# Attention over edges in order of target: a group of 14 tiles as two halves of 64 rows

## The reference

```python
xp = (x @ lin_w).reshape(N, HEADS, HEAD_DIM)
a_i = jnp.einsum('nhc,hc->nh', xp, att_i)
a_j = jnp.einsum('nhc,hc->nh', xp, att_j)
alpha = a_i[dst] + a_j[src]
alpha = jnp.where(alpha >= 0, alpha, NEG_SLOPE * alpha)
amax = jax.ops.segment_max(alpha, dst, num_segments=N)
ex = jnp.exp(alpha - amax[dst])
denom = jax.ops.segment_sum(ex, dst, num_segments=N)
alpha = ex / (denom[dst] + SOFTMAX_EPS)
msg = xp[src] * alpha[:, :, None]
out = jax.ops.segment_sum(msg, dst, num_segments=N)
...
out = (out - mu) * jax.lax.rsqrt(var + LN_EPS) * ln_w + ln_b
out = jax.nn.elu(out)
return out + x
```

## Time and profile before

| what | us |
|---|---|
| median of 3 runs | 4499.56 |
| lowest, highest | 4498.87, 4500.8 |
| span of the profiled execution | 5824.1 |
| PE busy, in it | 4650.5 |
| DVE busy | 3605.8 |
| POOL busy | 3218.0 |
| ACT busy | 1536.9 |
| mean granted clock of TensorE | 0.863 |

### The profile page before, as it was taken

The page is one execution under the profiler, slowest core; times in us unless marked ns, Lnnn a source line. Parts: engine busy times, 40 slices in busy tenths (PEclk is TensorE's granted clock), DMA queues, the critical chain, the costliest instruction groups (busy, mean ns, idle before and its releaser), DMA issues. The chain is left out here.

```text
span 5824.1 us, 116189 instructions
## 1 busy us (share of the span) xinstructions
PE 4650.5 (80%) x33992; PEld 2943.9 (51%) x33992; DVE 3605.8 (62%) x10598; ACT 1536.9 (26%) x3203; POOL 3218.0 (55%) x3385
## 2 busy tenths in 40 slices
PE   6888888888888888888847777777777777777777
PEld 4444444444444444444435665555556555565555
DVE  3566666666666666666526666666666666666666
ACT  3121222212222222222213333333333333333333
POOL 3555555555555555555445555555555555555552
PEclk8999999999999999999967777777777777777777
DMA  6444444444444444444433333333333333333331
GB/s 228 126 127 122 132 125 127 129 123 135 122 130 127 125 132 122 130 126 124 135 94 95 90 93 94 93 92 91 94 92 91 94 93 93 93 92 94 95 92 52
DMA packets 410283, 649.87 MB, mean 112 GB/s; under 512 B 138008, under 2 KB 270442, under 8 KB 410204
## 3 DMA queue, kind: packets, MB, share of 16 engines
q0 software_dynamic: 161120, 444.76, 27.5%
q1 hardware_dynamic: 249084, 204.19, 11.6%
HBM read 546.95 MB, written 101.68 MB: 111 GB/s over the span
## 5 line engine op out<-in xcount | busy, mean ns | idle before, releaser
L977 POOL DMA_INDIRECT sub_xg<-y_rows,sub_meta x1668 | 1599.1, 959 | 1208.1 <-PE sub_a L1027 558.7
L2342 POOL DMA_INDIRECT ord_xg<-xpa_rows,ord_meta x1666 | 1597.6, 959 | 1201.8 <-PE ord_a L2410 548.0
L2410 PE MATMUL ord_a<-ord_xg,ord_sel 128*128 128x264 f32 x3332 | 1330.0, 542 | 91.5 <-DVE ord_xg L2773 66.5
L1027 PE MATMUL sub_a<-sub_mids,sub_sel 128*32 128x128 f32 (+1 forms) x13344 | 1119.7, 312 | 311.8 <-issue 215.3
L2410 PEld LDWEIGHTS ord_a<-ord_xg,ord_sel 128*128 128x128 f32 x3332 | 834.9, 275 | 255.8 <-DVE ord_xg L2773 76.1
L1347 DVE TENSOR_TENSOR sub_mids<-sub_w,sub_xg 128x256 f32<-128x256 f32 x834 | 351.1, 421 | 983.7 <-remote 790.2
L1027 PEld LDWEIGHTS sub_a<-sub_mids,sub_sel 128*32 128x32 f32 x13344 | 463.0, 110 | 810.8 <-issue 545.8
L1352 DVE TENSOR_TENSOR sub_mids<-sub_w,sub_xg 128x384 f32<-128x384 f32 x1668 | 844.4, 548 | 0.0
L2358 PE MATMUL ord_s<-ident,ord_sel 128*128 128x128 f32 x1666 | 348.2, 337 | 569.7 <-ACT ord_sel_t L2476 539.6
L1007 PE MATMUL sub_w<-sub_fc,sub_ht 64*128 64x256 f32 x3336 | 611.8, 438 | 11.0 <-issue 10.7
L2358 PEld LDWEIGHTS ord_s<-ident,ord_sel 128*128 128x128 f32 x1666 | 244.3, 172 | 709.5 <-issue 684.5
(11 more groups left out here) (206 smaller groups left out, 4433.2 us busy)
## 6 DMA issues: line engine op xcount, KB each, us to landing
sub_sum_rows<-sub_agg_s SPq DMA_DIRECT2D x556, 64.0 KB
sub_node_rows<-sub_sum_rows SPq DMA_DIRECT2D x49, 640.0 KB, 5.6
sub_xg<-y_rows,sub_meta POOLq DMA_INDIRECT x1668
ord_xg<-xpa_rows,ord_meta POOLq DMA_INDIRECT x1666
ord_x_rows<-x_rows SPq DMA_DIRECT2D x119, 128.0 KB
out_dram<-ord_res SPq DMA_DIRECT2D x119, 128.0 KB
xpa_rows<-sub_proj SPq DMA_DIRECT2D x49, 264.0 KB, 2.2
lin_xt<-in_x_t_dram SPq DMA_DIRECT2D x14, 896.0 KB, 10.1
```

Of the source, the lines that this page charges most:

```text
L977: nc.gpsimd.indirect_dma_start(xg[:, b, k], None, y, bass.IndirectOffsetOnAxis(ids[:, b, 0, k:k + 1], 0))\
L1027: mm = nc.tensor.matmul(a[ROWS * m:ROWS * (m + 1), 0:w].rearrange("p (q f) -> p q f", f=MUL), sel[:, b, k, m], of, start=(j == 0), stop=False,
L2342: nc.gpsimd.indirect_dma_start(xg[:, b, k], None, xpa, bass.IndirectOffsetOnAxis(ids[:, b, k:k + 1], 0))\
L2410: mm = nc.tensor.matmul(psum_a[b % 2][:, 0:WIDE], sel[:, b, k], xg[:, b, k], start=(k == 0), stop=(k == TILES - 1 and not has(i, b, -1)), ...
```

## The change

The edges of a group are laid out as two halves of 896 edges (`by_halves`): tile k = 2j + s holds the edges of half s. A half's targets lie within 64 rows of the half's own first target (checked in `project_sources` with the other spans). The selection is 64 columns wide for each tile; the two halves' sums go to rows 0 to 63 and 64 to 127 of one bank. Two tiles side by side are transposed at once. A new product with a selection `pack` moves the rows to their node's place. The chain over partitions has 256 steps, and where it breaks is read from loaded targets (`att_ends`), not found and transposed.

```diff
@@ project_sources (set-up; DVE)
+                nc.vector.tensor_tensor(half_reach[:], half_last[:], half_first[:], ALU.subtract)\
+                    .then_inc(half_fitted, 1)
...
+                nc.vector.tensor_reduce(half_span[:], half_reach[:], AX, ALU.max).then_inc(half_fitted, 1)
...
+                nc.vector.tensor_scalar(c["spans"][:, -1:], half_span[:], float(WINDOW // HALF_ROWS), None,
+                                        ALU.mult).then_inc(half_fitted, 1)
@@ attend_in_order
-    PARTS = ((0, 4), (4, 8), (8, 11), (11, 14))
+    PARTS = ((0, 4), (4, 8), (8, 12), (12, 14))
+    TURNED = ((0, 4), (4, HALF))
-        sel = ph.sb("sel", [P, TURN, TILES, WINDOW])
-        sel_t = ph.sb("sel_t", [WINDOW, TILES, P])
+        sel = ph.sb("sel", [P, TURN, HALF, 2, HALF_ROWS])
+        sel_t = ph.sb("sel_t", [WINDOW, HALF, P])
+        pack = ph.sb("pack", [P, 2, WINDOW])
-        psum_a = [ph.ps(f"a{b}", [P, 512]) for b in range(2)]
+        psum_c = [ph.ps(f"c{b}", [P, 512]) for b in range(2)]
+        psum_a = ph.ps("a", [P, 512])
@@ SP
-                    at = start_of(g)
-                    sp.dma_start(ai[:, b], att[bass.ds(at, WINDOW), HEADS:2 * HEADS]).then_inc(meta_in[b], 16)
+                    sp.dma_start(ends[:, b].rearrange("h d c -> h (d c)"),
+                                 io["att_ends"][bass.ds(g, 1)].rearrange("o h c -> (o h) c")).then_inc(meta_in[b], 16)
+                    for n in range(2):
+                        at = sp.value_load(c["half_i"][0:1, bass.ds(2 * g + n, 1)], min_val=0, max_val=NODES_PAD)
+                        sp.dma_start(ai[HALF_ROWS * n:HALF_ROWS * (n + 1), b, HEADS * n:HEADS * (n + 1)],
+                                     att[bass.ds(at, HALF_ROWS), HEADS:2 * HEADS]).then_inc(meta_in[b], 16)
@@ POOL
-                        wait_alone(pool, meta_in[b], 32 * (i + 1))
+                        wait_alone(pool, meta_in[b], 64 * (i + 1))
@@ PE, turn_over
-                    for k in range(4 * q, min(TILES, 4 * q + 4)):
-                        last_mm = nc.tensor.transpose(psum_s[:, k % 4], sel[:, b, k], c["ident"][:])
+                    for n, j in enumerate(range(*TURNED[q])):
+                        last_mm = nc.tensor.transpose(psum_s[:, n], sel[:, b, j].rearrange("p s r -> p (s r)"),
+                                                      c["ident"][:])
@@ PE, spread
-                    for k in range(half * HALF, (half + 1) * HALF):
-                        last_mm = nc.tensor.matmul(psum_i[:, k * HEADS:(k + 1) * HEADS], sel_t[:, k], ai[:, b],
+                    for j in range(HALF):
+                        last_mm = nc.tensor.matmul(psum_i[:, j * 2 * HEADS:(j + 1) * 2 * HEADS], sel_t[:, j], ai[:, b],
@@ PE, turn_ends: the transpositions of broken go, the ends are four
-                        nc.tensor.transpose(psum_m[0:HEADS, 2 * d], of, c["ident"][:])
-                        last_mm = nc.tensor.transpose(psum_m[0:HEADS, 2 * d + 1], broken[:, d], c["ident"][:])
+                        for n in range(2):
+                            last_mm = nc.tensor.transpose(psum_m[0:HEADS, 2 * d + n], of[:, :, n], c["ident"][:])
@@ PE, hand_on
+                    wait_alone(pe, raw_done, g + 1)
@@ PE, add_up
-                    mm = nc.tensor.matmul(psum_a[b % 2][:, 0:WIDE], sel[:, b, k], xg[:, b, k], start=(k == 0),
-                                     stop=(k == TILES - 1 and not has(i, b, -1)), skip_group_check=True)
+                    j, n = k // 2, k % 2
+                    mm = nc.tensor.matmul(psum_c[b % 2][HALF_ROWS * n:HALF_ROWS * (n + 1), 0:WIDE], sel[:, b, j, n],
+                                          xg[:, b, k], start=(j == 0),
+                                          stop=(j == HALF - 1 and (n == 1 or not has(i, b, -1))),
+                                          skip_group_check=True)
+                def pack_rows(g, b, first):
+                    wait_alone(pe, placed, g + 1)
+                    wait_alone(pe, copied, g + 1)
+                    if not first:
+                        wait_alone(pe, pre_done, g)
+                    nc.tensor.matmul(psum_a[:, 0:WIDE], pack[:, b % 2], agg_s[:, b % 2], start=True, stop=True,
+                                     skip_group_check=True).then_inc(packed, 1)
@@ PE, order: pack_rows(g - 1) stands between hand_on and turn_ends at k == 2
-                            if k in (0, 3, 4, 6) and more:
+                            if k in (0, 4) and more:
-                            if k == 7 and more:
+                            if k == 8 and more:
                                 spread_chains(g + 1, after)
-                            if k == 8 and more:
+                            if k == 10 and more:
                                 ...
@@ ACT: two turn_out in place of four, after them shrink as before
+                def scale_ends(g, b, i, first):
...
+                    nc.scalar.activation(ends_f[:], ends[:, b], ACT.Copy, scale=NEG).then_inc(ends_scaled, 1)
@@ DVE
-                    nc.vector.tensor_tensor(sel[:, b], rel[:].unsqueeze(2).to_broadcast([P, TILES, WINDOW]),
+                    shape = [P, TILES, HALF_ROWS]
+                    nc.vector.tensor_tensor(sel[:, b].rearrange("p j s r -> p (j s) r"),
+                def place_rows(g, b, first):
+                    if not first:
+                        dve.wait_ge(packed, g - 1)
+                    nc.vector.tensor_scalar(pack[:, b % 2], c["ramp"][:], place[:, bass.ds(g, 1)], None, ALU.is_equal)\
+                        .then_inc(placed, 1)
-                    nc.vector.tensor_reduce(any_change[:], change[:], AX, ALU.max).then_inc(broke, 1)
-                    nc.vector.tensor_scalar(broken[:], any_change[:].unsqueeze(2).to_broadcast([P, 2, HEADS]), NEG,
-                                            None, ALU.mult).then_inc(prepared, 1)
+                def find_breaks(g):
+                    dve.wait_ge(ends_scaled, g + 1)
+                    nc.vector.tensor_tensor(broken[:], ends_f[:, :, 1:], ends_f[:, :, 0:CHAIN], ALU.subtract)\
+                        .then_inc(broke, 1)
-                    nc.vector.tensor_copy(broken_t[:], psum_m[0:HEADS, 1::2]).then_inc(started, 1)
@@ DVE, denominators
-                    dve.wait_ge(copied, g + 1)
+                    dve.wait_ge(packed, g + 1)
@@ DVE, order of a turn: weigh(g, b, 0), then
+                        if more:
+                            find_ends(g + 1)
+                            find_breaks(g + 1)
                         if past:
                             denominators(g - 1, before)
-                        if more:
-                            find_ends(g + 1)
```

More of the change, by code:

```diff
@@ L66 @@
 ATT_GROUPS = math.ceil(EDGES / GROUP)
+HALF_EDGES = HALF * P
+HALF_ROWS = WINDOW // 2
+HALVES = 2 * GROUPS
 HIDDEN_AT, COPY_AT, ADD_AT = 7, 1, 4
@@ L2379, in turn_ends @@
                         wait_alone(pe, best_done, g)
[L2380 to L2382 removed]
+                    for d, of in enumerate((ahead[:, :, :, HALF], back[:, :, :, 1])):
+                        for n in range(2):
+                            last_mm = nc.tensor.transpose(psum_m[0:HEADS, 2 * d + n], of[:, :, n], c["ident"][:])
                     last_mm.then_inc(ends_turned, 1)
@@ L2517, in turn @@
                         take_own(0, 0, 0, True)
-                        for q in range(QUARTS):
+                        scale_ends(0, 0, 0, True)
+                        for q in range(2):
                             turn_out(0, q, True)
@@ L2527, in turn @@
                         if has(i, b, -1):
-                            copy_out(g - 1, (b - 1) % TURN)
+                            copy_out(g - 1, (b - 1) % TURN, i if b > 0 else i - 1)
                         if more:
                             take_own(g + 1, after, after_i, False)
-                            for q in range(QUARTS):
+                            scale_ends(g + 1, after, after_i, False)
+                            for q in range(2):
                                 turn_out(g + 1, q, False)
@@ L2561, in _ @@
                 nc.vector.memset(mean_var[:], 1.0).then_inc(set_up, 1)
+                nc.vector.memset(ai[:], 0.0).then_inc(zeroed, 1)
                 nc.vector.memset(zeros[:], 0.0).then_inc(zeroed, 1)
                 dve.wait_ge(set_up, 8)
-                nc.vector.tensor_copy(ramp, c["ramp"][:]).then_inc(set_up, 1)
+                nc.vector.tensor_copy(ramp, c["ramp"][:, 0:HALF_ROWS]).then_inc(set_up, 1)
                 nc.vector.tensor_tensor(step_f[:, 1:], c["start_b"][:, 1:], c["start_b"][:, 0:GROUPS - 1],
                                         ALU.subtract).then_inc(stepped, 1)
-                dve.wait_ge(stepped, 1)
-                dve.wait_ge(numbered, 1)
-                nc.vector.tensor_scalar(hand[:, 1:], step_f[:, 1:], row_no[:], None, ALU.is_equal)\
+                dve.wait_ge(numbered, 2)
+                for n in range(2):
+                    part = slice(HALF_ROWS * n, HALF_ROWS * (n + 1))
```

(9 more changed lines are left out.)

241 lines of the change are left out of this document (144 added, 97 removed).

## The result

The kernel after takes 4570.93 us (median of 4 runs, 4566.95 to 4572.84), the kernel before 4499.22 us beside it: a ratio of 1.0154 (95% interval 1.0140 to 1.0168; the two medians by themselves give 1.0159). It is slower by 72 us where 50 us less were predicted. The profiled execution took 4569.8 us, close to the runs. That of before took 5824 us, so the fair partner for it is a second profile of the unchanged kernel before: 4499.6 us.

A forecast was written before the change was run, and what follows sets the result against it. The kernel was taken to run close to POOL's gathers, 17.66 us a group; DVE's turn 16.9 - 0.15 + 1.0 = 17.75, taken as 17.85 against 18.3: -54 us, +5 set-up, about 4450 us, range 4375 to 4515.

The forecast's parts named there:

- 75 us of excess: Whole kernel: median of the runs above gathers plus ends; placed in the attention, 0.63 us a group over POOL's 17.66.
- the three ends: Stretches without gathers: 87 us before the first, 59 between the stages, 78 after the last, taken as in the profile.
- rival (a): Attention already at the gathers' pace, the 75 us in convolution and ends; 4491 to 4508 us; chance 0.17.
- 4425 us: Whole kernel: both stages' gathers at 1.26 us (2100 and 2098 us) plus the ends and two single gathers.
- 0.45 us a turn: Attention group: gain from 18.3 us before to 17.85 after, times 119 groups, -54 us.
- the wait for `packed`: New DVE wait at the denominators for PE's layout product: 0.7 to 2.2 us a group, taken as 1.0.
- rival (b): DVE waits 2.2 us at the denominators, PE at half clock; turn 18.95 us, total 4582 us; chance 0.12.
- The cover: DVE's work during the wait for the product: two scans of `find_ends` and `find_breaks`, 1.6 us.
- the carry's wait: DVE's wait for ACT's `shrink` at the carry: 3.0 us a group, expected to go nearly whole.
- rival (c): PE's column tiles do not overlap, 28 full pitches stay; DVE's wait milder than rival (b), 4515 us; chance 0.05.
- (d): Gathers quicker than 1.26 us outside the profile, attention bound by DVE, ACT and PE; 4200 to 4370 us; chance 0.08.
- the 0.34 us taken: PE: price of each switch of array shape; 13 a group instead of 6, so 2.4 us more.

The follow-up runs named there:

- e0: The kernel before, unchanged, run again for a second profile: 4501.04 us, a profiled span of 4499.6 us.
- f2: The kernel before with two of the fourteen row gathers of an attention group left out: 4473.5 us, ratio 0.9935, turn 17.32 us.
- g3: The kernel after with ten products of no use put on PE ahead of a group's first sums: 4632.0 us, ratio to before 1.0291.
- e1: The kernel after with denominators, invert and divide moved behind the second weighing on DVE: 4514.2 us, ratio to before 1.0017.
- f1: The kernel after with the division behind the second weighing on DVE and the layout product ahead of the hand-on on PE: 4508.7 us, ratio to before 1.0013.
- f3: The kernel after with two of the fourteen row gathers of an attention group left out: 4576.0 us, ratio to before 1.0159, turn 18.15 us.
- e3: The kernel before with one more 128x1024 product (1.22 us) on DVE in each group: 4686.4 us, ratio 1.0396, turn 19.10 us.

## Why the prediction was wrong

**The step that failed first: how 75 us of excess were placed.** The prediction put all of it into the attention, with the three ends as in a profile that was itself disturbed, and so had 18.3 us a turn before. It is 17.56 in the runs. Of the excess over 4425 us, the convolution has 100 us, the gap between the stages 7 (66 for 59), the attention's gathers 4, and the shorter end gives 35 back. That was rival (a), given 0.17: the attention was already at the gathers' pace, and nothing could be gained by shorter work on any other engine. The 0.45 us a turn of the sum did not exist; e0 and f2 show it.

**The second: the wait for `packed` taken at 1.0 us.** The bounds, 0.7 to 2.2, held 2.14, and the value taken from their lower part was the wrong one. It was rival (b), whose price for this term was right to 0.06 us, given 0.12. Its own condition stood in the prediction (less work leaves more pauses and the clock falls) and came true: 0.85 to 0.67. The prediction took the value that went with the full clock; the 2.3 to 2.9 us put down for that are 1.92 us (g3), and the 3.8 us at half clock are 3.38. The cover, put at 1.6 us, is 1.28. So both terms of the difference were too long by about as much, and that 2.2 came so near is in part luck. (b)'s total, 4582, came near 4571 since its turn (18.95) and its base (18.3) were both some 0.8 us too long, so that their difference, 0.65, was close to the measured 0.56: luck too.

The two do not weigh the same. With the first alone the change would have given nothing: with 1.0 us in place of 2.14 the turn redone below is 16.99 us, under the gathers' 17.66. e1 and f1, where this wait is gone, are that case, 4514 and 4509 us, and inside the range stated. It is the second that made the kernel slower and put the time outside.

**The sum, redone with measured terms.** Free turn before 17.32 (f2). From f2 to f3, between 2500 and 4400 us and for a group: DVE's work -0.05 (1668.28 us at 17.32 a turn against 1586.88 at 18.15); the carry's wait -0.94 (102.8 / 109), where the prediction had 3.0 go, from rows that the disturbance had stretched; the old wait at the denominators -0.21; that for the chain ends -0.13; the new one +2.14. That is 18.13, and f3 measured 18.15. Against the gathers' 17.66, not against 17.32, only 0.5 us of it shows a turn, 66 us in all with the last turns.

**What was right.** DVE's work hardly moved: -0.05 us a group from f2 to f3 and -0.09 from e0 to after, for -0.15 predicted. Its larger parts are right too:

```profile
L2666 DVE TENSOR_TENSOR ord_sel<-ord_rel,ord_dve 128x896 f32<-128x896 f32 x104 | 113.1, 1088 | 13.3
...
L2724 DVE TENSOR_TENSOR_SCAN ord_chain_f<-ord_broken,ord_chain_f,ord_m 8x256 f32<-8x256 f32 x104 | 76.4, 734 | 14.2
...
L2697 DVE TENSOR_TENSOR ord_broken<-ord_ends_f 8x512 f32<-8x512 f32 x105 | 68.8, 656 | 0.0
L2727 DVE TENSOR_TENSOR_SCAN ord_chain_b<-ord_broken,ord_m 8x256 f32<-8x256 f32 x104 | 67.5, 649 | 0.0
```

`sel` 1.09 us for 1.05 predicted, `find_breaks` 0.66 for 0.69, the two chain scans +0.53 (0.734 + 0.649 less 0.468 + 0.382) for +0.5. The column tiles do overlap: in 1661 of the 1666 pairs the second pass of the sums starts under 0.02 us after the first, as in none of e0's, and the sums keep PE busy 604 us in the window against 1030 before, with 28 passes a group in both, so rival (c) is out. The gathers kept their pitch, so (d) is out. The convolution did not move. The switch ahead of the hand-on costs more than the 0.34 us taken: the weight load stands 0.40 us idle at full clock (g3) and 0.78 at half (after), where e0 has 0.345 and 0.68. But fewer of them show than were counted: weight loads that wait over 0.25 us for nothing that the profile shows are about 6 a group in e0 and 8 after, not 6 and 13, though some may lie within other waits. The Trainium skill, "TensorEngine Tiling (Array Packing)", Key Properties, has the drain without a price; the trace agrees in that the delay stands where the shape changes, and its price here follows the clock. The profiled span expected, 5450 to 5700 us, was wrong because the disturbance it was scaled from did not recur; the +5 us of set-up were about 4, all between the stages: 10.5 us from the convolution's last store to the attention's first gather in after, 6.3 in e0, and no later start of the convolution (85.4 and 86.5 us).

## What to carry to other kernels

A profile that is 29% longer than the runs is no base for a difference of 1%: take another one first, and until then count the rhythm of the engine that the disturbance doesn't touch, stage by stage. Where an engine's loop lies 0.3 us under another's, work taken off it is worth nothing, while a wait put into it is charged above those 0.3 us. A product placed between two steps of a loop costs its whole queue on the other engine at the clock that engine will then have; put it first in that queue, or move its reader behind work that doesn't need it.

## What the runs showed of the hardware

A switch of the array's shape costs with the clock (0.40 and 0.78 us from 64 columns to one). Added products in PE's pauses did not give the full clock throughout: with ten no pause of PE between 2500 and 4400 us was over 1.1 us, yet the granted clock was 0.73 in mean; with six it was 0.69. Over the chain from the first sums to the denominators it was full in none of 105 turns after, in 26 of 104 with six, and in 53 of 102 with ten. PE's waits with ten:

```profile
PE ord_c L2450 <- DVE ord_xg L2866: 162.5, 202, 1.1
PE ord_m L2426 <- DVE ord_chain_b L2731: 81.8, 101, 0.8
```

PE is busy 1434 us of the 1900 in after (clock 0.67), 1648 with six, 1655 with ten and 1741 in e0 (0.85). The Trainium skill, "TensorE: Matmul & The Clock Gate", Part 1, has the clock follow how busy the array has lately been; this order agrees. But e3, the kernel before with more work on DVE, has 0.85 with PE busy for 1620 us, less than with six or ten, and with pauses of PE up to 4.5 us:

```profile
2500.00:4400.00 1900.00, 1620.15 (x8111) 1189.47 (x8110) 1618.14 (x4550) 741.59 (x1485) 1373.95 (x1406) 0.85 0.42 115
```

So neither the absence of pauses nor PE's busy time over the whole stretch tells the clock here; what does is open.

A gather engine that runs a ring ahead hides the loss in its own rows: over the attention's gathers POOL is idle 525.4 us after and 510.9 in e0, and ends only 33 us later (4489.12 against 4456.13), while the kernel ends 70 us later. From the last gather to the end it is 80.7 us after and 43.5 in e0: the last groups' rows are there and wait for DVE.

```profile
4489.12 0.95 POOL L2378 DMA_INDIRECT ord_xg<-xpa_rows,ord_meta  x1 [0.30 <-issue]
```
